# Rounding repair of two 8-bit quantisation chains: a sign-and-magnitude form with more comparisons

## What is computed

```python
def _quant_input(x):
    s = 127.0 / jnp.clip(jnp.max(jnp.abs(x), axis=-1, keepdims=True), 1e-05, None)
    return jnp.clip(jnp.round(x * s), -128.0, 127.0) / s

xq = _quant_input(x)                       # 2048 features per token
x13 = jnp.einsum('bsd,fd->bsf', xq, w13)
x1, x3 = jnp.split(x13, 2, axis=-1)
gated = jnp.square(jax.nn.relu(x1)) * x3
inner = _rmsnorm(gated, norm_w, NORM_EPS)  # 5632 features per token
iq = _quant_input(inner)
out = jnp.einsum('bsh,dh->bsd', iq, w2)
```

## Time and profile before

| what | us |
|---|---|
| median of 2 runs | 14087.82 |
| the two runs | 14032.48, 14143.17 |
| the profiled execution's own time | 14066.42 |
| its span (core 3, the slowest) | 14064.6 |
| spans of the 8 cores | 13969.4 to 14064.6 |

### The profile page before, as it was taken

One profiled execution on the slowest core, in us unless ns is written; L12 is line 12 of the kernel. 1 busy time (PEld: TensorE's weight loads), 2 busy tenths in 40 slices (PEclk: granted clock), 3 DMA queues, 4 the chain that ended last, 5 costly groups with the idle time before them and its releaser, 6 DMA issues. The chain is left out here.

```text
span 14064.6 us, 54762 instructions; the slowest of 8 cores (13969.4 to 14064.6 us)
## 1 busy us (share of the span) xinstructions
PE 7238.4 (51%) x20459; PEld 2119.1 (15%) x20459; DVE 4291.5 (31%) x6146; ACT 1604.2 (11%) x2521; POOL 955.9 (7%) x816
## 2 busy tenths in 40 slices
PE   3375555666666666666665223346676660404224
PEld 1131111111111111111111001112222220201102
DVE  4435454211111111122111332232222236353442
ACT  0000000111111111111111000000000002121111
POOL 0000000000000000000000111111101101010110
PEclk8687777555555555555555566668888875757667
DMA  3232222000000000000001122211111110404224
GB/s 77 68 89 77 69 78 83 11 11 12 11 12 11 12 11 11 11 21 11 12 2 33 39 37 54 53 21 32 31 30 32 31 23 15 96 22 88 62 47 95
DMA packets 291554, 542.69 MB, mean 39 GB/s; under 512 B 91420, under 2 KB 190937, under 8 KB 270809
## 3 DMA queue, kind: packets, MB, share of 16 engines
q0 software_dynamic: 32192, 198.19, 7.9%
q1 hardware_dynamic: 245017, 311.64, 7.1%
q10 hardware_dynamic: 14080, 29.37, 0.7%
HBM read 617.74 MB, written 119.54 MB: 52 GB/s over the span
## 5 line engine op out<-in xcount | busy, mean ns | idle before, releaser
L1418 PE MATMUL o_ps<-iqT,w_sb 128*128 128x512 bf16 x2816 | 666.4, 402 | 1783.5 <-DMA w_sb<-w2w 1783.5
L826 PE MATMUL av_ps<-probs,vh 128*128 128x512 bf16 x1280 | 777.8, 608 | 1243.5 <-DVE probs L818 636.3
L818 DVE TENSOR_TENSOR probs<-probs,mask_sb 128x512 bf16<-128x512 bf16 x512 | 217.7, 425 | 3751.3 <-ACT probs L810 3751.3
L810 ACT ACTIVATE probs<-sc_ps,negc_bc 128x512 bf16<-128x512 f32 x1280 | 881.2, 688 | 3526.7 <-PE sc_ps L804 3526.7
L1196 PE MATMUL f_ps<-xqT,w_sb 128*128 128x512 bf16 x2816 | 899.6, 491 | 484.4 <-DMA w_sb<-w3w 484.4
L797 PE MATMUL sc_ps<-qTn,kTn 128*128 128x512 bf16 x1280 | 777.0, 607 | 0.0
L943 PE MATMUL o_ps<-at_sb,ow_sb 128*128 128x512 bf16 x1024 | 360.3, 530 | 803.3 <-DMA at_sb<-attnT_s 471.3
L804 PE MATMUL sc_ps<-qTr,kTr 64*128 64x512 bf16 x1280 | 773.1, 604 | 0.0
L835 PE MATMUL r_ps<-probs,ones_st 128*1 128x512 bf16 x1280 | 747.9, 584 | 0.0
L1207 PE MATMUL f_ps<-xqT,w_sb 128*128 128x512 bf16 x2816 | 636.5, 379 | 0.0
L1418 PEld LDWEIGHTS o_ps<-iqT,w_sb 128*128 128x128 bf16 x2816 | 285.9, 103 | 2165.1 <-DMA w_sb<-w2w 1800.8
(11 more groups left out here) (257 smaller groups left out, 7207.8 us busy)
## 6 DMA issues: line engine op xcount, KB each, us to landing
w_sb<-w2w POOLq DMA_DIRECT2D x64, 1408.0 KB, 12.2
xnb_t<-x_nat SPq DMA_DIRECT2D x32, 1024.0 KB, 7.1
xtb_c<-xT SPq DMA_DIRECT2D x128, 256.0 KB, 2.9
ow_sb<-ow POOLq DMA_DIRECT2D x64, 512.0 KB, 6.1
w_sb<-w1w POOLq DMA_DIRECT2D x44, 512.0 KB, 5.6
w_sb<-w3w POOLq DMA_DIRECT2D x44, 512.0 KB, 7.4
gw_s<-gw_t SPq DMA_DIRECT2D x176, 128.0 KB, 1.8
gw_c<-gw_s SPq DMA_DIRECT2D x176, 128.0 KB, 2.1
```

Of the source, the lines that this page charges most:

```text
L810: ex = p.op("s", lambda e, bank=bank, slot=slot: e.activation(probs[slot][:], sc_ps[bank][:], AF.Exp, bias=negc_bc[:], scale=1.0), deps=[m ...
L826: e.matmul(av_ps[:], vh[par][:, ci * 128:(ci + 1) * 128], probs[slot][:], start=(ci == 0), stop=(ci == n - 1), skip_group_check=True), dep ...
L1418: stop = p.op("t", lambda e, kc=kc, wp=wp: e.matmul(o5_ps[wp][:], w2_sb[wp][:, kc * 128:(kc + 1) * 128], iqT[:, kc * 512:(kc + 1) * 512], ...
```

## The change

Three edits:

- P3's repair takes the form that P5's has. VectorE's four steps on the difference `d` and the last one with its `-2.0` (five operations of the form scalar_tensor_tensor) go. In their place ScalarE takes the absolute value into `yq` and the sign into `d_t`, and VectorE makes a first comparison with 0.5, three more with 1.5, 2.5 and 3.5, a product with the sign, a sum with the integer, and a product with the inverse scale.
- P5's list of further thresholds grows from four to seven (5.5, 6.5 and 7.5 are new).
- The constant `SCALE` is worked out in float32 on the host; it goes into the kernel as an immediate, as before.

```diff
-SCALE = 1.0 / math.sqrt(192.0)
+SCALE = float(np.float32(1.0) / np.float32(np.sqrt(np.float32(192.0))))
...
-                        aa = p.op("v", lambda e, cp=cp: e.scalar_tensor_tensor(
-                            a_t[cp][:], d_t[cp][:], 0.5, r0_t[cp][:],
-                            ALU.is_gt, ALU.add), deps=[dd])
-                        aa = p.op("v", lambda e, cp=cp: e.scalar_tensor_tensor(
-                            a_t[cp][:], d_t[cp][:], 1.5, a_t[cp][:],
-                            ALU.is_gt, ALU.add), deps=[aa])
-                        bb = p.op("v", lambda e, cp=cp: e.scalar_tensor_tensor(
-                            b_t[cp][:], d_t[cp][:], -0.5, a_t[cp][:],
-                            ALU.is_ge, ALU.add), deps=[aa])
-                        bb = p.op("v", lambda e, cp=cp: e.scalar_tensor_tensor(
-                            b_t[cp][:], d_t[cp][:], -1.5, b_t[cp][:],
-                            ALU.is_ge, ALU.add), deps=[bb])
+                        ab = p.op("s", lambda e, cp=cp: e.activation(
+                            yq[cp][:], d_t[cp][:], AF.Abs), deps=[dd])
+                        sg = p.op("s", lambda e, cp=cp: e.activation(
+                            d_t[cp][:], d_t[cp][:], AF.Sign), deps=[ab])
+                        cm = p.op("v", lambda e, cp=cp: e.tensor_single_scalar(
+                            a_t[cp][:], yq[cp][:], 0.5, ALU.is_gt), deps=[ab])
+                        for thr in (1.5, 2.5, 3.5):
+                            cm = p.op("v", lambda e, cp=cp, thr=thr:
+                                      e.scalar_tensor_tensor(
+                                          a_t[cp][:], yq[cp][:], thr, a_t[cp][:],
+                                          ALU.is_gt, ALU.add), deps=[cm])
+                        co = p.op("v", lambda e, cp=cp: e.tensor_tensor(
+                            b_t[cp][:], a_t[cp][:], d_t[cp][:], ALU.mult),
+                            deps=[cm, sg])
+                        rf = p.op("v", lambda e, cp=cp: e.tensor_tensor(
+                            b_t[cp][:], b_t[cp][:], r0_t[cp][:], ALU.add), deps=[co])
                         xq = p.op("v", lambda e, dc=dc, cp=cp, gc0=gc0:
-                                  e.scalar_tensor_tensor(
+                                  e.tensor_tensor(
                                       xqT[:, dc * MYT + gc0:dc * MYT + gc0 + 512],
-                                      b_t[cp][:], -2.0, si_bc[:], ALU.add, ALU.mult),
-                                  deps=[bb, bsi])
+                                      b_t[cp][:], si_bc[:], ALU.mult),
+                                  deps=[rf, bsi])
...
-                        for thr in (1.5, 2.5, 3.5, 4.5):
+                        for thr in (1.5, 2.5, 3.5, 4.5, 5.5, 6.5, 7.5):
```

## The result

| | before | after |
|---|---|---|
| median, us | 14088.34 (10 runs) | 14602.01 (11 runs) |
| range, us | 14032 to 14143 | 14533 to 14701 |
| profiled execution: time | 14066.42 | 14639.64 |
| profiled execution: span | 14064.6 (core 3) | 14638.1 (core 1) |

The ratio is 1.0367, with a 95% interval of 1.0337 to 1.0398: 514 us slower by the medians, 475 to 561 us by the interval. The sum of the prediction was 495.1 us. Some executions of each kernel are slower, with a lower granted clock on some of the cores; they are left out of all times and ratios here. The two profiled executions alone differ by 573 us, which is outside that interval; what the other 78 us are is the open question that several of the experiments go after.

A forecast was written before the change was run, and what follows sets the result against it. Serial chains of waits in P3 and P5, set by the order of VectorE's list, were taken to bound the kernel. P5's 375.0 and P3's 120.1 us added to 14066.4 gave 14561.5 us, range 14510 to 14650.

The forecast's parts named there:

- The sum of the prediction: Whole kernel: 375.0 us from P5 plus 120.1 us from P3, 495.1 us on the profiled 14066.4.
- Serial chains, so each added operation counts: P3 and P5: tiles don't overlap, so added time counts per tile; periods 10.78 and 11.63 us.
- The hop to ScalarE in P3: P3's tile: new form passes through ScalarE, 1.29 + 0.66 us, within a growth of 1.84 us per tile.
- The last tile of a block: P5: last tile ends 3.66 us before the weights arrive, so covered; 43 tiles count per block.
- the 16 loads behind the sign: P3's block end: `at_sb` loads issued 2.64 us later, 7.9 us over three changes of block.
- Tables of ScalarE: P3: no table switching, 0 us; rival of one switch each way per block, 10.3 us, chance 0.09.
- The rival of "something dearer, such as transfers on which cores now meet": Both chains: one more us per tile on 240 tiles would make 14801; chance 0.03.
- The rival in which it gives time back: P4: half of its 484.4 us weight waits goes as cores spread, giving 14319.5 us; chance 0.02.

The follow-up runs named there:

- Experiments 1 and 2: P3's edit alone (kernel after with P5's old list): ratio 1.0072; P5's edit alone (kernel before with the longer list): ratio 1.0273.
- experiment 5: Twice the dose: kernel after with three more comparisons in P5 (8.5, 9.5, 10.5), eleven in all; one execution of 15139 us.
- experiment 7: Kernel after with the next tile's first operations written ahead of this tile's comparisons in both chains; ratio 0.9935 to the kernel before.
- experiment 6: Kernel after with the next `ow` load issued one output tile earlier in GpSimd's list; ratio 1.0102 to the kernel before.
- experiment 8: Kernel after with both chains' tiles overlapped and loads of `ow`, `w1`, `w3` and a block's first two `w2` issued earlier; 13200 us, ratio 0.9346.
- experiment 10: Kernel after with overlapped chains, early weights, GpSimd's chain operations on VectorE, next tile's subtraction between this tile's comparisons; 12972 to 13136 us, ratio 0.9234.

## Why the prediction was right

**Serial chains, so each added operation counts.** Right. The tiles are 11.62 and 10.78 us for 11.63 and 10.78. Experiments 1 and 2 add up to what the sum has, 120 and 377 us of stage time for 120.1 and 375.0 (that P3's agrees to the microsecond is partly luck, as its mean scatters by 58 us between executions of equal code); the dose test has the same price for a comparison when there are twice as many. That the reason is the order of VectorE's list, and not VectorE's work, is shown by experiment 7: tiles shrink to 9.27 and 8.02 us when that order alone is changed.

**The hop to ScalarE in P3.** Right, and it was worth working out: by VectorE's operations alone (two more, one of them short) the tile would have grown by 1.2 us, and the other 0.6 would have been missed. The rows of P5's chain, same shapes, gave every part of it. The prediction calls the hop nearly half of the 1.84 us; by its own rows it is 1.29 + 0.66 us where there were 1.30 before, so 0.65 us, about a third. The sum doesn't use that share.

**The last tile of a block.** Right in P5 that it doesn't count, but the cover is deeper than the 3.66 us to the weights' arrival, "and no more", that the prediction gave it: experiment 5 went up to 1.0 us beyond them, beside the first 44 matmuls, and nothing waited. In P3 the step on what is late next, the 16 loads behind the sign, was right to 0.5 us: the wait grew by 30.7 us, and the sum had 15 x 1.84 + 2.64 = 30.2.

**Tables of ScalarE.** Right to take none: one load in P3. The page "ScalarE: Activation LUTs" of the Trainium skill, section "Table sets: the hidden batching unit", warns of a change of set, and names one set with both exponential and logarithm. The trace agrees for these two, and adds that the sign is to be had in the loaded set without a second load.

**What the sum had no term for.** The profiled execution after lies 78 us above the sum, and by the means of the cores 56 us of that are in P3, 12 in P5 and 11 in P4; no run explains the last two. The rival of "something dearer, such as transfers on which cores now meet" had the right kind of thing, and wrong on one point: it isn't caused by the change. P3 with its old code took 1655, 1657 and 1713 us in three executions, with its new code 1832, 1803, 1775 and 1784 in four; the means differ by 1798 - 1675 = 123 us, which is the sum's 120 within that scatter. The stage scatters by as much as half the edit's effect, on both kernels, since its weight loads are uncovered (experiment 6). The difference of the medians, 514 us, has 19 us of it left, and the interval holds the sum. The median of 14602 us lies 41 above the stated likeliest of 14561; 21 of these come from starting at a profiled execution that was itself below the median, as the prediction says. The prediction read the earlier trace rows for what waits in P5 and at `at_sb`, but did not read the 332.0 us of `ow` waits in P3 as a place where executions can differ; its range, from the two runs of before and the covers, was wide enough all the same.

**P4.** The rival in which it gives time back had no part: with the statistics behind it, it took 2327 us before and 2338 after on the mean of the cores (2354 and 2330 in the second executions). The rival also had more to give back than there was: of its 484.4 us the first wait, 157.7, is TensorE standing idle while P3's last chain ends, and it grew with that chain, so that the total is 514.4 us in the kernel after.

## What to carry to other kernels

Low busy shares on every engine are no room for more work where each engine's list has the next tile behind the end of this one: follow one tile through the timeline, add up the new operations with their gaps and hops between engines, and multiply by the tiles whose end something waits for. Before the arithmetic is cut, change the order of the lists: here 610 us came from writing the next tile's first operations ahead of this tile's last, and 830 more (experiments 7 to 8, by the ratios) from writing weight loads ahead of an operation that waits. Where a list takes over an operation that waits for another engine, put enough of its own work between; and one profiled execution doesn't price a small edit where loads are uncovered, so compare each stage on all cores and in a second execution before a difference is explained.

## What the runs showed of the hardware

VectorE and GpSimd hindered one another where both worked on tiles in SBUF at once, in the overlapped chains and in P4 of every kernel. A comparison with two tile inputs took up to 1.761 us in place of 0.692 in experiment 8, P3's first comparison (one tile input) 1.49 in place of 0.43, both about 1.07 us more; GpSimd's subtraction in P5 took 1.52 us on the mean in place of 1.26. With GpSimd out of the chains the comparisons are back at 692 and 420 ns. The Trainium skill has this in "SBUF — State Buffer", section "Who interferes with whom": VectorE's instructions with two SBUF inputs, or in a mode that uses both ports, share a port pair with GpSimd's reads, and the second to start waits. The traces agree: GpSimd, which starts within a comparison, loses 0.27 us, and the next comparison up to 1.07 us, most of a GpSimd operation. It means here that a GpSimd operation of 1.26 us beside VectorE takes 0.94 us from it, more than the 0.73 us that VectorE needs to do it itself.

ScalarE did copy, logarithm, exponential, absolute value and sign in P3 of the kernel after with one table load of 1.283 us.

In several executions, of kernels old and new, two or four cores took 20 to 150 us longer than the others in P4. In experiment 10 these cores had a granted clock of 0.82 there (core 0, P4 and statistics 2018 us) where the others had 0.91 (core 4, 1888 us). Which cores it meets changes from one execution to the next, and no run here shows what lowers it.
